# Computing the cross-attention's values in the attention's first batch instead of in the preparation

## The chip, the cores and the metric

The kernel runs on one core of a Trainium2 chip. The metric is the time of one execution on the device in microseconds, the median of several runs. The profile is of one execution; its span runs from the first to the last instruction.

## What is computed

One decoder layer over x of 8 x 512 x 512, with a context of 8 x 77 x 512. Three sublayers stand one behind the other, each with a residual and a layer norm: a mixing of tokens in the frequency domain, a cross-attention with 16 heads onto the context, and a dense layer whose weights are first rounded to 4 bits.

```python
qkv = x @ w_qkv                                     # 8 heads of 64
kv = cumsum(fft(k) * fft(v), axis=1)
x = layernorm(x + ifft(kv * conj(fft(q))).real @ w_out)

q, k, v = x @ W_q + b_q, ctx @ W_k + b_k, ctx @ W_v + b_v     # 16 heads of 32
attn = softmax(where(mask == 0, -1e6, q @ k.T / sqrt(32)))
x = layernorm(x + (attn @ v) @ W_o + b_o)

w = clip(round(kernel / scale), -8, 7) * scale      # scale = max|kernel| / 7
x = layernorm(x + x @ w + bias + (x @ a) @ b)
```

## The kernel before, in words

All matrix products take float32 apart into a high and a low piece, so that a product is three matmuls per 128 rows of the contraction (`split_matmuls`, L130). ScalarE makes the high piece by a copy, VectorE or GpSimd the low one by a subtraction. There are three blocks, each ended by a barrier of all engines. Within a block every engine has its own list of work, written out by hand, and waits on semaphores. All DMAs are issued by SyncE, in the order of its list.

**Preparation** (`prepare`, L134 to L484). TensorE turns the context (616 rows, kept as `ctxT`, two pieces), then makes the keys in 8 products of 308 columns and the values in 5 products of 12 matmuls with 512 columns (4 of 128 rows, `tiles`, and one of 104). ScalarE and VectorE cut each product into its pieces in four slots, `out_hi` and `out_lo`, from which SyncE stores it to DRAM (`keys_split`, `values_split`). A slot is used again once its store has landed. Then come 12 folds: w_qkv is turned and multiplied by the Fourier matrix, which gives `w_spec`, and at the end `w_back` from w_out. A fold's product needs one of two banks, which VectorE frees when it has made the low piece (`split_folded`, L454). Between these, VectorE quantizes the dense layer's weights: the greatest absolute value of `kernel` (L443, behind the fourth value tile), then three passes. After the sixth fold it begins to turn x of the first batch (L92), which it waits for. GpSimd makes the low pieces of W_v.

**Mixing** (`mix_tokens`). 8 batches over two tiles for x. At its end TensorE turns the mixed first batch (`x1`) and projects it to queries, VectorE and GpSimd (`root`, L761) finish the last batch's layer norm, and SyncE loads the first keys.

**Attention** (`attend`). A step is a batch: 8 scores (four tiles of 128 tokens, two halves of the heads), softmax, the turning of the probabilities in three banks per tile (P00 to P32), the turning of the next batch's x1 (X0 to X3) and its queries (Q0 to Q3), and of the batch before: weighing the values (V), W_o (O), turning (T), the dense layer (F). Scores have banks of their own; everything else goes through a ring of 4 banks (`shared_ps`), whose order the lists `START_ORDER` and `BANK_ORDER` give: `Shared` works out from them which bank a use has and which earlier one must be empty (`freed`, counted by VectorE). The first batch (step 0) has only scores, P, X and Q. For a tile ScalarE runs 16 exponentials (`exponentials`, L1413), 8 per half, each half behind VectorE's maximum (L1719, L1724), and the next tile's score in that half waits for them.

SyncE's list in step 0 is: the values of batch 0 (`load_values`, L1114, 12 small DMAs per piece into the block-diagonal `v_block`), then the keys of batch 1 (`load_next_keys`, L517, 8 DMAs), then the residual. The first score of batch 1 waits for these keys:

```python
def load_values(i):
    wait_reuse(sp, oT_hi, i * NC)
    for part in range(2):
        for odd, j, m, row, key, n in v_pieces():
...
...
pe.wait_ge(k_loaded, nth(i, 1, 0) * (16 * 2 * GH))
```

Of the kernel before, what the change touches and what calls it, by code (L numbers as in the profile page):

```python
# [18 lines left out]
F32 = mybir.dt.float32  # L19
# [6 lines left out]
P = 128  # L26
# [20 lines left out]
QMAX = 7.0  # L47

# [85 lines left out]
def prepare(nc, ins, constants, half_power, ident, w_spec, w_back, k_dram, v_dram, ffn_dram, x_first, hand, ffn,  # L134
            out_slots, w_k, w_v):
# [4 lines left out]
    rows = B * KEYS  # L140
    half_rows = rows // 2
    tiles = [(n * P, min(P, rows - n * P)) for n in range((rows + P - 1) // P)]
    tail, tail_rows = tiles[NC]
    with ExitStack() as ctx:  # L144
# [13 lines left out]
        raw_v = wqkv_sb[:].rearrange("p c n -> p (c n)")[:, NC * D:2 * NC * D].rearrange("p (c n) -> p c n", c=NC)  # L158
# [13 lines left out]
        ctx_loaded, wk_loaded, wv_loaded = sem("ctx_loaded"), sem("wk_loaded"), sem("wv_loaded")  # L172
# [4 lines left out]
        wk_hi_ready, wk_lo_ready, wv_hi_ready, wv_lo_ready = sem("wk_hi_ready"), sem("wk_lo_ready"), sem("wv_hi_ready"), sem("wv_lo_ready")  # L177
        prod_ready, prod_used = sem("prod_ready"), sem("prod_used")
        k_biased, k_hi_ready, k_lo_ready = sem("k_biased"), sem("k_hi_ready"), sem("k_lo_ready")
        v_hi_ready, fold_hi_ready = sem("v_hi_ready"), sem("fold_hi_ready")  # L180
        stored = [sem(f"kv_stored{n}") for n in range(SLOTS)]
# [6 lines left out]
        NKEY, NVAL = 2 * NC, len(tiles)  # L188
# [18 lines left out]
        def _(sp):  # L207
# [8 lines left out]
            sp.dma_start(raw_v, by_chunk(ins["W_v"])).then_inc(wv_loaded, 16)  # L216
            sp.dma_start(fwd[:], ins["dft_forward"]).then_inc(fwd_loaded, 16)
            load_interleaved(sp, wqkv_sb, ins["w_qkv"], 0, qkv_loaded[0])
            for n in range(NKEY):
# [6 lines left out]
                if n == NC + 1:  # L226

                    sp.wait_ge(tail_turned, NC)
                    sp.wait_ge(a_turned, 1)
                    sp.dma_start(ffn[:], by_chunk(ins["kernel"])).then_inc(kernel_loaded, 16)  # L230
                elif 1 <= n < NC:

                    sp.wait_ge(wv_lo_ready, NC)
                    load_interleaved(sp, wqkv_sb, ins["w_qkv"], n, qkv_loaded[n])
            for n, (at, size) in enumerate(tiles):
                sp.wait_ge(prod_used, AT_V + n + 1)
                for part, tile in enumerate((out_hi, out_lo)):
                    sp.dma_start(v_dram[part, at:at + size, :], tile[0:size, n % SLOTS, :].bitcast(F32)).then_inc(stored[n % SLOTS], 16)
                if n == 1:

                    sp.wait_ge(wk_lo_ready, NC)
                    sp.dma_start(wout_sb[:], by_chunk(ins["w_out"])).then_inc(out_loaded, 16)

# [11 lines left out]
            for n in range(SLOTS):  # L255
                sp.wait_ge(stored[n], 32 * (NKEY // SLOTS + len(range(n, NVAL, SLOTS))))
# [4 lines left out]
        def _(pe):  # L261
# [29 lines left out]

            pe.wait_ge(wv_hi_ready, 1)
            pe.wait_ge(wv_lo_ready, NC)
            for m, (at, size) in enumerate(tiles):
                n = AT_V + m
                pe.wait_ge(prod_used, n - 1)
                pieces = [([t[:, k, at:at + size] for t in ctxT], [w[:, k, :] for w in w_v]) for k in range(NC)]
                split_matmuls(nc, prod[n % 2][0:size, :], pieces).then_inc(prod_ready, 1)
# [46 lines left out]
        def _(act):  # L345
# [10 lines left out]
            act.wait_ge(wv_loaded, 16)  # L356
            nc.scalar.activation(w_v[0][:], raw_v, ACT.Copy).then_inc(wv_hi_ready, 1)
# [5 lines left out]
            for m, (at, size) in enumerate(tiles):  # L363
                act.wait_ge(prod_ready, AT_V + m + 1)

                act.wait_ge(stored[m % SLOTS], 32 * (NKEY // SLOTS + m // SLOTS))
                nc.scalar.activation(out_hi[0:size, m % SLOTS, :], prod[(AT_V + m) % 2][0:size, :], ACT.Copy).then_inc(v_hi_ready, 1)

# [22 lines left out]
        def _(pool):  # L391
            nc.gpsimd.memset(half_power[:], -0.5)
            pool.wait_ge(wv_loaded, 16)
            pool.wait_ge(wv_hi_ready, 1)
            for c in range(NC):
                nc.gpsimd.tensor_tensor(w_v[1][:, c, :], raw_v[:, c, :], w_v[0][:, c, :].bitcast(F32),
                                        ALU.subtract).then_inc(wv_lo_ready, 1)
# [4 lines left out]
        def _(dve):  # L402
# [31 lines left out]
            for m, (at, size) in enumerate(tiles):  # L434
                dve.wait_ge(v_hi_ready, m + 1)

                dve.wait_ge(stored[m % SLOTS], 32 * (NKEY // SLOTS + m // SLOTS))
                nc.vector.tensor_tensor(out_lo[0:size, m % SLOTS, :], prod[(AT_V + m) % 2][0:size, :],
                                        out_hi[0:size, m % SLOTS, :].bitcast(F32), ALU.subtract).then_inc(prod_used, 1)

                if m == 3:
                    dve.wait_ge(kernel_loaded, 16)
                    nc.vector.tensor_reduce(top[:], ffn[:].rearrange("p c n -> p (c n)"), AX.X, ALU.max,  # L443
                                            apply_absolute_value=True).then_inc(top_ready, 1)
                if m == 4:
# [75 lines left out]
def mix_tokens(nc, x, x1_dram, k_dram, mask_dram, ident, sigma, w_spec, w_back, half_power, w_q_dram, w_q, bias_q, hand):  # L521
# [4 lines left out]
    with ExitStack() as ctx:  # L526
# [50 lines left out]
        def _(sp):  # L577
# [32 lines left out]
            for i in range(B - 3, B - 1):  # L610
                finish(i)
# [144 lines left out]
        def _(pool):  # L756
# [59 lines left out]
            for t in range(NT):  # L816
                root(B - 1, t)
# [1237 lines left out]
```

## Time and profile before

| | |
|---|---|
| median of 3 runs | 937.67 us (936.75 to 938.23) |
| the profiled execution | 939.91 us |
| its span | 937.3 us |
| busy: TensorE / VectorE / ScalarE / GpSimd | 885.3 (94%) / 654.1 (70%) / 369.1 (39%) / 360.4 (38%) |
| mean granted clock of TensorE | 0.978 of full speed |
| bytes written to DRAM / read | 22.87 MB / 52.60 MB |

The execution's own time is 2.6 us more than its span; that part lies outside of what the trace shows. On the trace's clock the preparation ends at about 93 us and the attention block begins at about 456.8 us.

### The profile page before, as it was taken

The page shows a single profiled execution, that of the slowest core. Times are in us where ns is not written, and L with a number is a line of the kernel's source. Part 1 is how long each engine was busy: PE and PEld are TensorE (multiplying, and loading weights), DVE is VectorE, ACT ScalarE, POOL GpSimd, SP SyncE. Part 2 cuts the span into 40 slices and gives each one's busy share as a digit, 9 for nine tenths or more (in the row PEclk, how much of TensorE's full clock was granted, in tenths as well). Part 3 has the DMA queues.
Part 4 walks back from the last instruction along what each step waited for, and adds up shares of the span by engine and source line. Part 5 has one row for each costly group of instructions (what it writes and reads, how often), then busy time and mean ns, then how long its engine had stood idle before and what let it go on. Part 6 is the DMA issues. An engine that isn't in the chain of part 4 may idle for free.

```text
span 937.3 us, 14606 instructions
## 1 busy us (share of the span) xinstructions
PE 885.3 (94%) x4284; PEld 733.8 (78%) x4284; DVE 654.1 (70%) x1133; ACT 369.1 (39%) x1403; POOL 360.4 (38%) x338
## 2 busy tenths in 40 slices
PE   4798999999999999999689999999999999999887
PEld 4683888888888888888578888888888888888775
DVE  2355456666666657567667977879778797887957
ACT  3152221112121211101387555755556646566611
POOL 1000365434353544315236444335443353434523
PEclk9997999999999999999879999999999999999999
DMA  6871720312314020104513141321403114030021
GB/s 184 261 227 45 167 58 34 102 62 74 92 43 133 12 79 23 67 24 133 190 25 99 23 123 31 98 66 25 136 13 96 66 30 134 11 94 18 19 79 45
DMA packets 85962, 76.02 MB, mean 81 GB/s; under 512 B 39895, under 2 KB 58583, under 8 KB 85919
## 3 DMA queue, kind: packets, MB, share of 16 engines
q1 hardware_dynamic: 85919, 75.49, 27.4%
q8 instruction: 21, 0.34, 0.2%
q14 instruction: 22, 0.18, 0.1%
HBM read 52.60 MB, written 22.87 MB: 81 GB/s over the span
## 4 chain that ended last, share of the span: by engine, by line
PE 44%; DVE 5%; issue 2%; ACT 1%; DVEq 0%; POOLq 0%; POOL 0%; ACTq 0%
PE shared_ps L130 33%; PE score_ps L130 5%; PE shared_ps L1206 3%; PE shared_ps L1168 1%; PE shared_ps L1239 1%; DVE xT_lo L1677 1%; DVE score_ps L1719 1%; DVE x_and_res L1765 1%; ACT probs L1413 1%; DVE pT_lo L1704 0%; DVE stats L1749 0%; DVE top_s L1724 0%; DVE y L1743 0%; DVE hidden L1710 0%; DVE y_out L1765 0%
## 5 line engine op out<-in xcount | busy, mean ns | idle before, releaser
L1413 ACT ACTIVATE probs<-score_ps,top_s 128x77 f32<-128x77 f32 x512 | 158.9, 362 | 28.5 <-DVE top_s L1724 28.5
L1413 ACT ACTIVATION_READ_ACCUMULATOR probs<-score_ps,top_s 128x1 f32 x512 | 124.7, 245 | 0.0
L1562 POOL TENSOR_TENSOR probs<-probs,per_total 128x616 f32<-128x616 f32 x64 | 79.1, 1253 | 67.1 <-DVE per_total L1731 66.9
L1555 POOL TENSOR_TENSOR rstd<-ve,half_power 128x1 f32<-128x1 f32 x64 | 35.0, 547 | 154.5 <-DVE ve L1754 149.4
L100 POOL TENSOR_TENSOR xT_lo<-x_tok,xT_hi 128x512 fp32r<-128x512 f32 x28 | 39.0, 1396 | 85.7 <-ACT xT_hi L96 85.7
L729 ACT ACTIVATE qT_hi<-vals 128x512 fp32r<-128x512 f32 x32 | 19.3, 628 | 119.1 <-POOL vals L776 103.8
L776 POOL TENSOR_TENSOR vals<-qs_prod 128x512 f32<-128x512 f32 x32 | 40.9, 1290 | 62.7 <-DVE qs_prod L862 62.7
L1420 ACT ACTIVATE pT_hi<-shared_ps 128x512 fp32r<-128x512 f32 (+1 forms) x96 | 47.6, 539 | 42.0 <-PE shared_ps L1206 41.8
L722 ACT ACTIVATE v_sb<-v_ps 128x512 f32<-128x512 f32 x32 | 18.9, 594 | 106.8 <-PE v_ps L130 106.8
L1577 POOL TENSOR_TENSOR x_and_res<-x_and_res,bias_f 128x512 f32<-128x512 f32 x32 | 41.7, 1302 | 43.9 <-DVE x_and_res L1765 30.1
L1719 DVE COPY_PREDICATED score_ps<-hidden,score_ps 128x616 f32<-128x616 int32 x64 | 50.9, 796 | 10.9 <-PE score_ps L130 10.6
L761 POOL TENSOR_TENSOR mix_rstd<-mix_ve,half_power 128x1 f32<-128x1 f32 x32 | 21.9, 686 | 94.4 <-DVE mix_ve L881 94.4
L1704 DVE TENSOR_TENSOR pT_lo<-shared_ps,pT_hi 128x512 fp32r<-128x512 f32 (+1 forms) x96 | 56.0, 595 | 0.5 <-issue 0.3
L130 PE MATMUL shared_ps<-w_ffn_hi,xT_hi 128*128 128x512 f32 x120 | 49.2, 410 | 7.4 <-DVE xT_lo L1677 6.0
L130 PE MATMUL shared_ps<-w_o_hi,xT_hi 128*128 128x512 f32 x128 | 53.4, 417 | 1.9 <-DVE xT_lo L1685 1.8
L1724 DVE TENSOR_REDUCE top_s<-score_ps 128x8 f32<-128x616 f32 x64 | 51.2, 799 | 3.6
L130 PE MATMUL v_ps<-xT_hi,w_spec_hi 128*128 128x512 f32 x128 | 49.9, 390 | 1.8 <-PEq L144 1.8
L130 PE MATMUL score_ps<-xT_hi,qT_hi 128*128 128x308 f32 x128 | 42.5, 332 | 9.7 <-ACT probs L1413 7.5
L130 PE MATMUL shared_ps<-w_o_lo,xT_hi 128*128 128x512 f32 x128 | 51.0, 398 | 0.0
L130 PE MATMUL shared_ps<-w_o_hi,xT_lo 128*128 128x512 f32 x128 | 50.8, 397 | 0.0
L130 PE MATMUL v_ps<-xT_hi,w_spec_lo 128*128 128x512 f32 x128 | 49.8, 389 | 0.0
L130 PE MATMUL v_ps<-xT_lo,w_spec_hi 128*128 128x512 f32 x128 | 49.8, 389 | 0.0
(210 smaller groups left out, 2637.0 us busy)
## 6 DMA issues: line engine op xcount, KB each, us to landing
x_tok<-in_x SPq DMA_DIRECT2D x32, 256.0 KB, 4.6
x_res<-in_x SPq DMA_DIRECT2D x8, 1024.0 KB, 7.6
x_between<-mix_x SPq DMA_DIRECT2D x32, 256.0 KB, 2.0
x<-x_between SPq DMA_DIRECT2D x8, 1024.0 KB, 5.5
x_tok<-x_between SPq DMA_DIRECT2D x8, 1024.0 KB, 5.6
out<-y_out SPq DMA_DIRECT2D x32, 256.0 KB, 2.0
wqkv_sb<-in_w_qkv SPq DMA_DIRECT2D x16, 192.0 KB, 5.6
keys_split<-w_q_hi SPq DMA_DIRECT2D x8, 154.0 KB, 5.4
```

Source lines behind the costliest of these rows:

```text
L100: engine.tensor_tensor(blocks(xT[1][:, j, :]), block_column(tile, j), blocks(xT[0][:, j, :]).bitcast(F32), ALU.subtract).then_inc(lo_ready, 1)
L130: last = nc.tensor.matmul(out, l, r, start=(n == 0), stop=(n == len(terms) - 1))
L776: nc.gpsimd.tensor_tensor(vals[:, h, :], qs[:, 2 * h, :], qs[:, 2 * h + 1, :], ALU.subtract if h else ALU.add).then_inc(vals_summed, 1)
L1206: last = nc.tensor.transpose(shared_ps[s.bank(use)][0:size, n * P:(n + 1) * P], probs[:, t % 2, at:at + size], ident[:])
L1413: nc.scalar.activation(probs[:, t % 2, j * KEYS:(j + 1) * KEYS], score_ps[:, g, k * KEYS:(k + 1) * KEYS], ACT.Exp, bias=top[:, t % 2, j:j ...
L1420: nc.scalar.activation(pT[0][0:size, first:first + chunks, t * P:(t + 1) * P], turned_bank(s, t, c), ACT.Copy).then_inc(turned_hi, 1)
L1555: nc.gpsimd.tensor_tensor(rstd[:, n:n + 1], ve[:, n:n + 1], half_power[:], ALU.pow).then_inc(rstd_ready, 1)
L1562: nc.gpsimd.tensor_tensor(p, p, per_total[:, t % 2, h * heads:(h + 1) * heads].unsqueeze(2) .to_broadcast([P, heads, KEYS]), ALU.mult).the ...
L1577: nc.gpsimd.tensor_tensor(res2[:, t % 2, :], x2[:, t % 2, :], bias_f[:], ALU.add).then_inc(res2_ready, 1)
L1704: nc.vector.tensor_tensor(lo, turned_bank(s, t, c), hi.bitcast(F32), ALU.subtract).then_inc(freed, 1)
L1719: nc.vector.copy_predicated(s4, hidden[:, t, :].unsqueeze(1).unsqueeze(1).to_broadcast(shape), masked[h].unsqueeze(1).unsqueeze(1).to_broa ...
L1724: nc.vector.tensor_reduce(top[:, t % 2, h * 8:(h + 1) * 8].rearrange("p (g j) -> p g j", j=GH), s4, AX.X, ALU.max, negate=True).then_inc(t ...
```

## The change

Preparation: W_v is no longer loaded or cut apart, and the 5 value products, their copies and their stores are gone. All of w_qkv is loaded at the start, w_out right behind it. The turned context `ctxT`, both pieces, is stored to DRAM (`ctx_turned`, 2 DMAs) behind the last key store and ahead of x. `top` stands before the folds, the scale behind the second fold, the first pass behind the third.

Mixing: W_v is loaded into `x_tok0` before the last batch but one is finished. ScalarE copies its high piece behind the turning of the next x1, GpSimd makes the low pieces in four parts between the last roots. SyncE loads the turned context back (4 DMAs) behind the first keys, into the room of `w_spec`, which now lives on into the attention and holds `w_o`, `w_ffn` and `v_block` too.

Attention, first batch: the value products W0 to W4 take their place in the ring. ScalarE and VectorE cut each into `pT`, SyncE stores it (10 DMAs) and waits until all have landed; then come `load_values` and the keys of batch 1 as before.

```diff
-        AT_V = NKEY
-        AT_FOLD = AT_V + NVAL
+        AT_FOLD = NKEY
...
             sp.dma_start(a_sb, by_chunk(ins["a"])).then_inc(a_loaded, 16)
-            sp.dma_start(raw_v, by_chunk(ins["W_v"])).then_inc(wv_loaded, 16)
             sp.dma_start(fwd[:], ins["dft_forward"]).then_inc(fwd_loaded, 16)
-            load_interleaved(sp, wqkv_sb, ins["w_qkv"], 0, qkv_loaded[0])
+            for r in range(NC):
+                load_interleaved(sp, wqkv_sb, ins["w_qkv"], r, qkv_loaded[r])
+            sp.wait_ge(wk_lo_ready, NC)
+            sp.dma_start(wout_sb[:], by_chunk(ins["w_out"])).then_inc(out_loaded, 16)
...
-            for n, (at, size) in enumerate(tiles):
-                sp.wait_ge(prod_used, AT_V + n + 1)
-                for part, tile in enumerate((out_hi, out_lo)):
-                    sp.dma_start(v_dram[part, at:at + size, :], tile[0:size, n % SLOTS, :].bitcast(F32)).then_inc(stored[n % SLOTS], 16)
+            sp.wait_ge(ctx_hi, 2 * NC)
+            sp.wait_ge(ctx_lo, 2 * NC)
+            for part, tile in enumerate(ctxT):
+                sp.dma_start(ctx_dram[part], tile[:].bitcast(F32)).then_inc(ctx_stored, 16)
...
-            for m, (at, size) in enumerate(tiles):
-                dve.wait_ge(v_hi_ready, m + 1)
...
-                if m == 3:
-                    dve.wait_ge(kernel_loaded, 16)
+            dve.wait_ge(kernel_loaded, 16)
+            nc.vector.tensor_reduce(top[:], ffn[:].rearrange("p c n -> p (c n)"), AX.X, ALU.max,
+                                    apply_absolute_value=True).then_inc(top_ready, 1)
...
+            sp.dma_start(x_tok[0][:], w_v_dram.rearrange("(c p) n -> p c n", p=P)).then_inc(wv_loaded, 16)
+            finish(B - 2)
...
+            sp.wait_ge(q_filled, nth(B - 1, 4, 3))
+            for part in range(2):
+                for into, cols in zip(hand.ctxT(w_spec), (slice(0, S), slice(S, CTX_ROWS))):
+                    sp.dma_start(into[part].bitcast(F32), ctx_dram[part, :, :, cols]).then_inc(hand.ctx_loaded, 16)
             store(B - 1)
...
-START_ORDER = ["P00", "P01", "P02", "X0", "X1", "X2", "X3", "P10", "P11", "P12", "Q0", "P20", "P21", "Q1",
-               "P22", "Q2", "P30", "P31", "P32", "Q3"]
+START_ORDER = ["W0", "W1", "W2", "P00", "P01", "P02", "W3", "X0", "X1", "W4", "P10", "P11", "P12", "X2", "X3",
+               "Q0", "Q1", "P20", "P21", "P22", "Q2", "P30", "P31", "P32", "Q3"]
...
+            for n, (at, size) in enumerate(CTX_TILES):
+                sp.wait_ge(freed, Shared(0, False, True, True).emptied(f"W{n}"))
+                for part in range(2):
+                    sp.dma_start(v_dram[part, at:at + size, :].rearrange("p (a n) -> p a n", a=2),
+                                 values_of(part, n).bitcast(F32)).then_inc(v_stored, 16)
+            sp.wait_ge(v_stored, 32 * len(CTX_TILES))
             step(0, False, True, True)
...
             score(0, s, 0, 0)
             score(0, s, 0, 1)
+            project_v(s, 0)
             score(0, s, 1, 0)
+            project_v(s, 1)
             score(0, s, 1, 1)
-            score(0, s, 2, 0)
+            project_v(s, 2)
             turn_probs(0, s, 0, 0)
             turn_probs(0, s, 0, 1)
             turn_probs(0, s, 0, 2)
+            score(0, s, 2, 0)
+            project_v(s, 3)
             turn_x1(1, s, 0)
+            turn_x1(1, s, 1)
             score(0, s, 2, 1)
-            turn_x1(1, s, 1)
+            project_v(s, 4)
```

How the lists move, first SyncE's in the preparation, from the last value stores on (before) and from the sixth key store on (changed). `w_q_hi` and `w_q_lo` are the slots, `x` is the tile that receives `kernel`, `x_tok` receives x:

```order
L242 DMA wout_sb<-in_w_out 128x4x512
L238 DMA values_split<-w_q_hi 128x512
L238 DMA values_split<-w_q_lo 128x512
L238 DMA values_split<-w_q_hi 128x512
L238 DMA values_split<-w_q_lo 128x512
L238 DMA values_split<-w_q_hi 104x512
L238 DMA values_split<-w_q_lo 104x512
L246 DMA x_tok<-in_x 32x16x128 x4
L249 DMA wqkv_sb<-in_dft_inverse 128x512
```

```order
L233 DMA x<-in_kernel 128x4x512
L226 DMA keys_split<-w_q_hi 128x308
L226 DMA keys_split<-w_q_lo 128x308
L226 DMA keys_split<-w_q_hi 128x308
L226 DMA keys_split<-w_q_lo 128x308
L238 DMA ctx_turned<-ctxT_hi 128x2464
L238 DMA ctx_turned<-ctxT_lo 128x2464
L241 DMA x_tok<-in_x 32x16x128 x4
L244 DMA wqkv_sb<-in_dft_inverse 128x512
```

Where x followed the last value store, it now follows two stores of 1232 KB each that stand directly behind the keys.

ScalarE's list at the attention's start, before and changed. `probs` are the exponentials, `pT_hi<-shared_ps 128x4x128` and `104x2x128` a tile's turned probabilities, `xT_hi` x1 of the next batch, `qT_hi` its queries, and `pT_hi<-shared_ps 128x2x256` (or `104x2x256`) the high piece of a value product:

```order
L1413 ACTIVATE probs,total<-score_ps,top_s 128x77 x40
L1420 ACTIVATE pT_hi<-shared_ps 128x4x128 x2
L1420 ACTIVATE pT_hi<-shared_ps 104x2x128
L1396 ACTIVATE xT_hi<-shared_ps 128x512
L1413 ACTIVATE probs,total<-score_ps,top_s 128x77 x8
L1396 ACTIVATE xT_hi<-shared_ps 128x512 x3
L1420 ACTIVATE pT_hi<-shared_ps 128x4x128 x2
```

```order
L1458 ACTIVATE probs,total<-score_ps,top_s 128x77 x8
L1446 ACTIVATE pT_hi<-shared_ps 128x2x256
L1468 ACTIVATE pT_hi<-shared_ps 128x4x128 x2
L1458 ACTIVATE probs,total<-score_ps,top_s 128x77 x8
L1468 ACTIVATE pT_hi<-shared_ps 104x2x128
L1446 ACTIVATE pT_hi<-shared_ps 128x2x256
L1458 ACTIVATE probs,total<-score_ps,top_s 128x77 x8
L1435 ACTIVATE xT_hi<-shared_ps 128x512 x2
L1446 ACTIVATE pT_hi<-shared_ps 104x2x256
L1458 ACTIVATE probs,total<-score_ps,top_s 128x77 x8
L1468 ACTIVATE pT_hi<-shared_ps 128x4x128 x2
```

The changed piece begins with tile 1's first half of exponentials and the copy of W2; ahead of it stand the two halves of tile 0, each with a value piece behind it (W0, W1). The last value piece (W4, 104 rows) stands behind five halves of exponentials and ahead of the sixth, and all of tile 1's turned probabilities stand behind that.

## Rows read from the trace of the kernel before

**Rows 1.** The page, part 2: TensorE's granted clock, in 40 slices of 23.4 us

```profile
PEclk9997999999999999999879999999999999999999
```

**Rows 2.** Stretches: length, busy us (instructions) by engine, clock, DMA share, GB/s

```profile
40.00:50.00 10.00, 5.26 (x13) 4.16 (x14) 1.57 (x3) 1.09 (x2) 0.00 (x0) 0.66 1.04 367
457.00:500.00 43.00, 32.02 (x153) 27.57 (x154) 28.50 (x46) 32.89 (x149) 12.73 (x11) 0.80 0.30 93
500.00:545.00 45.00, 44.15 (x240) 37.76 (x239) 38.68 (x73) 28.28 (x133) 26.45 (x24) 1.00 0.28 79
```

**Rows 3.** TensorE in the preparation: start, length, line, work, [idle before <- ended by]

```profile
33.71 0.40 PE L130 MATMUL prod<-xT_hi,ctxT_hi 128*128 128x512 f32 x1
...
44.74 0.80 PE L130 MATMUL prod<-xT_hi,ctxT_hi 128*128 128x512 f32 x1 [5.28 <-DVE w_q_lo L438]
...
49.60 0.49 PE L130 MATMUL prod<-xT_lo,ctxT_hi 128*128 128x512 f32 x1
...
55.51 1.04 PE L309 MATMUL turned<-ident,wqkv_sb 128*128 128x128 f32 x8
```

**Rows 4.** VectorE in the preparation, same columns

```profile
32.97 0.48 DVE L432 TENSOR_TENSOR w_q_lo<-wT_sb,w_q_hi 128x308 fp32r<-128x308 f32 x1 [0.23 <-DVE wT_sb L420]
...
54.16 2.27 DVE L443 TENSOR_REDUCE top<-x 128x1 f32<-128x2048 f32 x1
...
58.68 0.69 DVE L454 TENSOR_TENSOR w_spec_lo<-prod,w_spec_hi 128x512 fp32r<-128x512 f32 x1 [1.33 <-ACT w_spec_hi L385]
...
66.78 0.70 DVE L92 STREAM_TRANSPOSE x_tok<-x_tok 128x512 f32<-128x512 f32 x1
```

**Rows 5.** SyncE's queue in the preparation, same columns

```profile
37.88 0.39 SPq L230 DMA_DIRECT2D x<-in_kernel  x1
```

**Rows 6.** Stretches of 2 us in the preparation, same columns as rows 2

```profile
34.00:36.00 2.00, 2.00 (x10) 1.64 (x9) 0.45 (x1) 0.46 (x1) 0.00 (x0) 1.00 1.05 246
46.00:48.00 2.00, 2.00 (x6) 1.52 (x6) 0.00 (x0) 0.00 (x0) 0.00 (x0) 0.50 1.07 390
62.00:64.00 2.00, 2.00 (x20) 2.00 (x20) 0.72 (x2) 1.28 (x3) 0.00 (x0) 1.00 1.24 233
```

**Rows 7.** DMA issues: count, KB each, median us to landing

```profile
values_split<-w_q_lo SPq DMA_DIRECT2D x4, 256.0 KB, 2.8
...
x_tok<-in_W_o SPq DMA_DIRECT2D x1, 1024.0 KB, 5.2
...
xT_lo<-keys_split SPq DMA_DIRECT2D x8, 38.5 KB, 1.9
```

**Rows 8.** TensorE in the attention's first batch and at the second's start

```profile
457.18 0.41 PE L130 MATMUL score_ps<-xT_hi,qT_hi 128*128 128x308 f32 x1 [2.17 <-DVE score_ps L1672]
...
464.10 0.62 PE L130 MATMUL score_ps<-xT_hi,qT_hi 128*128 128x308 f32 x1 [4.94 <-ACT probs L1413]
...
499.92 0.30 PE L130 MATMUL score_ps<-xT_hi,qT_hi 128*128 128x308 f32 x1
```

**Rows 9.** SyncE's queue in the attention's first batch

```profile
461.31 10.49 SPq L1114 DMA_DIRECT2D v_block_hi<-values_split  x12
471.85 9.92 SPq L1114 DMA_DIRECT2D v_block_lo<-values_split  x12
...
487.76 1.85 SPq L517 DMA_DIRECT2D xT_lo<-keys_split  x4
```

**Rows 10.** ScalarE in the attention's first batch: its first exponential

```profile
461.49 0.33 ACT L1413 ACTIVATE probs<-score_ps,top_s 128x77 f32<-128x77 f32 x1 [5.75 <-DVE top_s L1724]
```

**Rows 11.** The mixing's end: ScalarE, GpSimd's last root, VectorE's last piece

```profile
446.89 0.69 ACT L752 ACTIVATE qT_hi<-k_ps,bias_q 128x512 fp32r<-128x512 f32 x1 [7.42 <-PE k_ps L130]
...
450.30 0.80 POOL L761 TENSOR_TENSOR mix_rstd<-mix_ve,half_power 128x1 f32<-128x1 f32 x1 [2.64 <-DVE mix_ve L881]
...
455.77 0.75 DVE L930 SCALAR_TENSOR_TENSOR qT_lo<-q_ps,bias_q,qT_hi 128x512 fp32r<-128x512 f32 x1 [1.97 <-ACT qT_hi L752]
```

**Rows 12.** The page, part 5: GpSimd's subtractions of 128x512 in the mixing

```profile
L100 POOL TENSOR_TENSOR xT_lo<-x_tok,xT_hi 128x512 fp32r<-128x512 f32 x28 | 39.0, 1396 | 85.7 <-ACT xT_hi L96 85.7
```

More of the change, by code:

```diff
@@ L47 @@
 QMAX = 7.0
+CTX_ROWS = B * KEYS
+CTX_TILES = [(n * P, min(P, CTX_ROWS - n * P)) for n in range((CTX_ROWS + P - 1) // P)]
 def nth(batch, per_batch, index):
@@ L131, in split_matmuls, with prepare @@
     return last
-def prepare(nc, ins, constants, half_power, ident, w_spec, w_back, k_dram, v_dram, ffn_dram, x_first, hand, ffn,
-            out_slots, w_k, w_v):
-    rows = B * KEYS
+def prepare(nc, ins, constants, half_power, ident, w_spec, w_back, k_dram, ctx_dram, ffn_dram, x_first, hand, ffn,
+            out_slots, w_k):
+    rows, tiles = CTX_ROWS, CTX_TILES
     half_rows = rows // 2
-    tiles = [(n * P, min(P, rows - n * P)) for n in range((rows + P - 1) // P)]
     tail, tail_rows = tiles[NC]
@@ L815, in _, with split_wv @@
                 nc.gpsimd.memset(tile.bitcast(F32), 0.0).then_inc(hand.keys_cleared, 1)
-            for t in range(NT):
-                root(B - 1, t)
+            def split_wv(c):
+                pool.wait_ge(wv_hi, 1)
+                pool.wait_ge(wv_loaded, 16)
+                nc.gpsimd.tensor_tensor(w_v[1][:, c, :], x_tok[0][:, c, :], w_v[0][:, c, :].bitcast(F32),
+                                        ALU.subtract).then_inc(hand.wv_lo, 1)
+            split_wv(0)
+            root(B - 1, 0)
+            split_wv(1)
+            root(B - 1, 1)
+            split_wv(2)
+            root(B - 1, 2)
+            root(B - 1, 3)
+            split_wv(3)
         @block.vector
@@ L995, in bank @@
     def bank(self, use):
-        return self.order.index(use) % RING
+        shift = 0 if self.order is START_ORDER else len(START_ORDER)
+        return (self.order.index(use) + shift) % RING
     def filled(self, use):
@@ L1180, in project_q, with project_v @@
                 split_matmuls(nc, shared_ps[s.bank(use)][:], pieces).then_inc(filled, 1)
+            def project_v(s, n):
+                use, (at, size) = f"W{n}", CTX_TILES[n]
+                if n == 0:
+                    pe.wait_ge(hand.wv_lo, NC)
+                    pe.wait_ge(hand.ctx_loaded, 16 * 4)
+                wait_reuse(pe, freed, s.reusable(use))
+                ctx_of = ctx_main if n < NC else ctx_rest
+                at = at % S
+                pieces = [([x[:, k, at:at + size] for x in ctx_of], [w[:, k, :] for w in w_v]) for k in range(NC)]
+                split_matmuls(nc, shared_ps[s.bank(use)][0:size, :], pieces).then_inc(filled, 1)
             def score(i, s, t, h):
```

194 lines of the change are left out of this document (105 added, 89 removed).

## The prediction

> **What bounds the kernel now.** I read the clock and the stretches first, then TensorE's list with its idle time, then the lists of those that ended it. TensorE is busy for 94% of the span, and its clock falls in the preparation's second half (the slice from 70 to 94 us) and at the change from mixing to attention (445 to 492 us) [rows 1]; from 40 to 50 us it was 0.66 too [rows 2]. In the attention's first batch it is busy for 32.0 of 43 us at a mean clock of 0.80; in the 45 us after that it is idle for 0.85 us [rows 2]. So what delays the second batch's start delays the end by as much, and what fills the first batch's holes is partly free. In the preparation the value products run from 33.71 to 55.51 us, where the first turning for the folds begins: 21.8 us, of which 5.28 us are a wait for a slot whose store is late, and the 12 matmuls after it ran at half clock, 44.74 to 49.9 us [rows 3], while the DMA engines moved 367 GB/s [rows 2]. The preparation then hangs on VectorE: its first fold piece is at 58.68 us, its first turning of x, behind the sixth fold, at 66.78 us, and it did not wait for x [rows 4]. From there to the block's end the lists are the same in both kernels.
>
> The bound of measurement is 0.2%, 1.9 us: below that I call it no change.
>
> **Term 1: the preparation.** The question is when VectorE can turn x. Three things lead there.
>
> (a) The keys. TensorE ends them at about 33.9 us as before. Their last slots waited for stores behind the w_qkv loads before; now these loads are issued first. The sixth low piece ends at 32.97 + 0.48 = 33.45 us [rows 4], and behind its two stores (0.8 us of issue) the load of `kernel` is issued at 34.4 instead of 37.88 us [rows 5]. The last key piece should be done at 35.6 us.
>
> (b) The maximum. A load of 1 MB that had company landed after 5.2 us [rows 7]; with two key stores ahead I add 1 us: 40.6 us. The maximum takes 2.27 us [rows 4], so 42.9 us. TensorE has made folds 0 and 1 by then and stands still from about 39.4 to 43.7 us, since VectorE has freed no bank. That is a wait like the one of 5.28 us, which left the clock at half for 4.9 us of matmuls (44.74 to 49.60) [rows 3]. At half clock a fold takes about 2.6 us, so two of them, and then two at the 1.35 us of the list before ((66.78 - 58.68) / 6): folds 0 to 5 are done at about 51.5 us.
>
> (c) x. It stands behind, from 34.4 us on, one pair of key stores not yet moved (0.32 MB), `kernel` (1.05), two more pairs (0.63) and the context's stores (2.52): 4.5 MB. At the 367 GB/s of the value stores' time [rows 2] they take 12.3 us, then x's 1.05 MB at the 233 GB/s of x's own loading [rows 6] 4.5 us, and 2 us until the last has landed (the 2.8 us of a value store less 0.7 us for its 256 KB) [rows 7]: 53.2 us.
>
> So x decides, at 53.2 instead of 66.78 us: **13.6 us less**. From both sides: with everything ahead of x at 246 GB/s [rows 6], 59.2 us and 7.6 us less; with 390 GB/s [rows 6] and no tail, x lands at 50.4 us, and the folds at full clock are done at 50 us: 16.4 us less. I take the middle rate, since the context's stores are nearest to the value stores, in direction and in size.
>
> **Edits I cost at nothing.** The 1 MB of W_v and 2.5 MB of context that are loaded while the mixing ends move beside TensorE, which is saturated there. The context is issued behind the first keys, at about 444 us; at 233 GB/s with 2 us of tail it lands at 457 us, and its first reader, W0, can start at 459. If that cover were gone, each microsecond past 461 would count. GpSimd's four parts of W_v (1.4 us each, [rows 12]) stand between the roots; the last root began at 450.30 us and the block ended with VectorE at 456.52 us [rows 11], so over 5 us of slack stand against at most 2 us of shift. ScalarE's copy falls in its 7.42 us without work ahead of its first piece of the queries [rows 11]. The residual of batch 6, now behind W_v in SyncE's queue, is read only in the middle of the next step.
>
> **Term 2: the attention's first batch.** Added are 60 matmuls at 0.2325 us (12 in 2.8 us, [rows 3] before the stall), 14.0 us, five copies on ScalarE and five pieces on VectorE (0.7 us each at most, as a piece of a fold, [rows 4]), ten stores and a wait on SyncE. Now the list: scores of tile 0 from 457.18 us [rows 8], done at 459. W0 until 461.7. The next score waits for the eight exponentials that begin at 461.49 [rows 10], until 464.1 as before [rows 8], 2.6 us a half; W1 to 467.8, score, W2 to 471.4, three turnings to 473.3, score, W3 to 477.0, X0, X1, score to 478.8, **W4 to 481.6**. ScalarE's copy ends at 482.4; VectorE stands in the maximum of tile 2's second half until 483.8 and frees W4 at 484.4. Two exits lead from there to the second batch.
>
> The keys: the last store is issued at 485.0 and lands after 2.8 us [rows 7], 487.8. Then the 24 value loads, 10.49 + 9.92 us of issue before, now at least 9.92 twice [rows 9]: 508.0. Then 8 key loads, 3.7 us, the last landing 1.9 us after its issue began [rows 7, 9]: **513.2 us**. Before, these 20 us began at 461.31 us and nobody waited for the keys, which had been issued by 489.6.
>
> TensorE's own way: tile 1's turnings, a score, X2 and X3, which need banks that VectorE frees only behind the sixth half of exponentials: TensorE is nearly idle from 485 to 492 us, so that Q0's 12 matmuls run at half clock, as in [rows 3]. Q0 to 497.4, score, Q1, tile 2's turnings, Q2, and tile 3's probabilities behind its own exponentials; Q3 ends at about 512.5 us.
>
> Both give 513, against 499.92 us for the second batch's first score before [rows 8]: **13.4 us more**. Bounds: if the chain to W4 were 3 us shorter and TensorE's holes smaller, 10 us more; if W4 is freed 3.5 us later, 17. Below, a perfect filling of the 11 us of holes and of the slow clock would cost nothing, but the keys' chain excludes it: even a W4 that is freed at 479 us gives 507.8, 8 us more.
>
> The Trainium skill, DMA: Bandwidth & Descriptors, "Issuing engines are not separate DMA queues", says that the time an engine needs to start a DMA is usually small beside the DMA. By that rule the keys would be there before 495 us, TensorE's own way would decide alone, and the term would be 12.6 instead of 13.4 us. The trace does not agree: here a DMA of 19 KB holds the queue for 0.85 us.
>
> **The sum.** -13.6 + 13.4 = -0.2 us on the span, 937.3 to 937.1; the profiled execution was 2.6 us longer than its span and 2.2 us above the median. On the median of 937.67: **937.5 us**.
>
> **The rivals.**
> - Faster. The DMA engines keep up: the context's stores run at 390 GB/s, x lands at about 51 us, and the first batch is not as slow, since value products between the scores keep the clock up and W4 is freed at 481.5: -15.6 + 10.5 = -5.1, 932.6 us. For it: the clock of 0.80 there [rows 2] and a first score that found a cold engine. Against: TensorE's hole at 485 to 492 us stays. The Trainium skill, TensorE: Matmul & The Clock Gate, "Why this matters for your kernels", asks for no idle gaps between bursts of matmuls; by that rule it would come out this way, and the 5.28 us gap with its slow matmuls agrees with it.
> - Slower. SyncE's chain takes the place of the slot wait: its 20 us of small loads now begin only when all five value tiles have landed. If W4 is freed 3.5 us later than I count, the keys land at 516.7 us; TensorE, done at 512.5, then waits 4.2 us, and the second batch starts at half clock, which costs 2.2 us as after the 5.28 us gap (4.9 us for what takes 2.8). -13.6 + 16.8 + 2.2 = +5.4, 943.1 us. It decides from the point at which the keys land 3.5 us behind Q3.
> - The products do not find their cover: the context lands only at about 464 us, behind x1's stores, and W0 holds up the second tile's score in TensorE's list: +2.5 us, 940.0 us.
>
> **How the numbers follow.** My forecast 0.33, faster 0.33, slower 0.30, late context 0.04. The two terms are opposed, of equal size, and each is known to 3 us, so the likeliest has its own range of 934.5 to 940.5. The range of 931 to 944 us takes in both rivals and their bounds but not term 1's 7.6 us. Of my forecast's 0.33, 0.25 lies within 0.2%, 0.04 on each side; the near ends of the rivals give 0.01 and 0.02 more: faster 0.36, same 0.28, slower 0.36.
>
> **What would show it.** VectorE's first turning of x at 53 us with a wait for x in front; no slot waits; the maximum at 40.6 us; the mixing unchanged in length; W4 freed at 484.4 us after the attention's start of 456.8 (27.6 us later); the value loads as a solid row of 20 us on SyncE's queue and, right behind, the keys; the second batch's first score 56 us behind the first score instead of 42.7. It is wrong if x waits for nothing, if that distance is under 52 or over 60 us, or if any stage after it changes its length.

## The result, and the profile after

The changed kernel takes 944.00 us (median of 4 runs, 942.05 to 944.52) against 937.94 us for the kernel before (4 runs, 936.75 to 938.23): 1.0057 times as long, 95% interval 1.0045 to 1.0070. Beside the experiments below it ran again, 941.79 us against 937.98: 1.0047, interval 1.0031 to 1.0064. So it is **slower, by 4 to 6 us**; the forecast was 937.5.

The first trace has a span of 942.7 us against 937.3. Four marks that both kernels have cut it into stages. TensorE's list gives three of them in the changed kernel (start, duration, engine, line, operation, tile, shape, count, idle time before it and what ended it):

```profile
81.32 0.47 PE L134 MATMUL v_ps<-xT_hi,w_spec_hi 128*128 128x512 f32 x1 [1.83 <-PEq L147]
...
446.29 0.41 PE L134 MATMUL score_ps<-xT_hi,qT_hi 128*128 128x308 f32 x1 [3.89 <-DVE score_ps L1725]
...
503.27 0.63 PE L134 MATMUL score_ps<-xT_hi,qT_hi 128*128 128x308 f32 x1 [3.63 <-DMA xT_lo<-keys_split]
```

They are the mixing's first product, the attention's first score and the second batch's first score. The fourth is the first load of the third batch's keys on SyncE's queue, at 538.33 us before and here at

```profile
544.24 1.76 SPq L501 DMA_DIRECT2D xT_hi<-keys_split  x4
```

In the kernel before, the mixing's first product is at

```profile
93.96 0.47 PE L130 MATMUL v_ps<-xT_hi,w_spec_hi 128*128 128x512 f32 x1 [1.83 <-PEq L144]
```

and the two scores at 457.18 and 499.92 [rows 8]. The lengths, in us:

| stage | before | after | difference | forecast |
|---|---|---|---|---|
| preparation, to the mixing's first product | 93.96 | 81.32 | -12.64 | -13.6 |
| mixing, to the attention's first score | 363.22 | 364.97 | +1.75 | 0 |
| first batch, to the second's first score | 42.74 | 56.98 | +14.24 | +13.4 |
| from there to the third batch's keys | 38.41 | 40.97 | +2.56 | 0 |
| rest of the span | 398.97 | 398.46 | -0.51 | 0 |
| span | 937.30 | 942.70 | +5.40 | -0.2 |

The two terms I had worked out are each within a microsecond. Most of the miss, 4.3 us, stands in two of the stages that I had put at nothing.

**Preparation.** VectorE's list after, to be held against [rows 4]:

```profile
41.47 2.29 DVE L411 TENSOR_REDUCE top<-x 128x1 f32<-128x2048 f32 x1 [5.58 <-DMA x<-in_kernel]
...
54.01 0.71 DVE L96 STREAM_TRANSPOSE x_tok<-x_tok 128x512 f32<-128x512 f32 x1 [1.14 <-DMA x_tok<-in_x]
```

The slot waits are gone, the maximum stands at 41.5 instead of behind the value products, and the first turning of x at 54.0 instead of 66.78, behind a wait for x.

**Mixing's end.** SyncE's queue, and the next write of VectorE into the two-tile buffer that x1's stores empty:

```profile
429.32 2.91 SPq L501 DMA_DIRECT2D xT_lo<-keys_split  x4
432.27 0.67 SPq L615 DMA_DIRECT2D w_spec_hi<-ctx_turned  x1
...
434.32 0.76 SPq L615 DMA_DIRECT2D xT_lo<-ctx_turned  x1
435.12 9.55 SPq L580 DMA_DIRECT2D x_between<-mix_x  x4
```

```profile
442.65 0.55 DVE L897 TENSOR_SCALAR mix_x<-mix_r,mix_mv,mix_rstd 128x512 f32<-128x512 f32 x1 [5.05 <-DMA x_between<-mix_x]
```

The four loads of the context are issued just ahead of x1's last stores. The first store's 256 KB stand behind 2.5 MB, and VectorE cannot write the third normalised tile before they have gone. One more tile and three remainders of the queries are queued behind that instruction; the last of them ends at 445.6 us. TensorE had ended its own list at 442.4 us: its wait before the first score is 3.89 us against 2.17 [rows 8].

**First batch and second batch's start.** SyncE's queue:

```profile
472.67 1.02 SPq L1171 DMA_DIRECT2D values_split<-pT_hi  x1
473.74 0.89 SPq L1171 DMA_DIRECT2D values_split<-pT_lo  x1
477.91 20.02 SPq L1130 DMA_DIRECT2D w_spec_lo<-values_split  x24
497.98 1.92 SPq L501 DMA_DIRECT2D xT_hi<-keys_split  x4
499.94 1.87 SPq L501 DMA_DIRECT2D xT_lo<-keys_split  x4
```

The solid row of 20 us is there, with the keys behind it. TensorE is done at 499.64 us and waits 3.63 us for them (the row at 503.27 above), and then runs at a slow clock. The stretches of the changed kernel (busy time and count of PE, its weight loads, DVE, ACT, POOL; then the granted clock, DMA share, GB/s):

```profile
503.00:509.00 6.00, 5.73 (x18) 4.91 (x19) 1.60 (x2) 0.17 (x1) 4.06 (x5) 0.55 0.91 330
509.00:520.00 11.00, 10.93 (x54) 9.15 (x53) 7.30 (x11) 8.29 (x43) 5.92 (x5) 1.00 0.11 29
```

The kernel before, in the first 6 us of its second batch:

```profile
500.00:506.00 6.00, 6.00 (x33) 5.21 (x32) 5.33 (x8) 3.66 (x18) 5.85 (x4) 1.00 0.62 192
```

At a granted clock of 0.55 (mostly the lower level, 1.2 of 2.4 GHz) TensorE starts 18 matmuls in 6 us instead of 33. The filler below shows that this is the +2.56 us.

### The profile page after: what moved, and what is told of

Its sections match the earlier page's. It is cut to its first block, busy times and chain, and to the rows that moved or that the text cites. A ratio compares the mean times of both kernels' runs of the same rounds, so it can differ in the third digit from the quotient of the medians.

```text
span 942.7 us, 14604 instructions
## 1 busy us (share of the span) xinstructions
PE 884.1 (94%) x4284; PEld 733.3 (78%) x4284; DVE 654.9 (69%) x1133; ACT 369.2 (39%) x1403; POOL 360.2 (38%) x338
## 4 chain that ended last, share of the span: by engine, by line
PE 43%; DVE 4%; SPq 2%; issue 2%; ACT 1%; DMA 1%; POOLq 0%; POOL 0%; DVEq 0%
PE shared_ps L134 33%; PE score_ps L134 5%; PE shared_ps L1240 3%; SPq L1130 2%; PE shared_ps L1191 1%; PE shared_ps L1273 1%; DVE xT_lo L1730 1%; DVE x_and_res L1825 1%; ACT probs L1458 1%; DVE score_ps L1779 1%; DMA values_split<-pT_lo 0%; DVE pT_lo L1764 0%; SPq L501 0%; DVE stats L1809 0%; DVE y L1803 0%
## 5 line engine op out<-in xcount | busy, mean ns | idle before, releaser
L134 PE MATMUL shared_ps<-w_spec_hi,xT_hi 128*128 128x512 f32 (+1 forms) x380 | 139.1, 408 | 9.7 <-DVE xT_lo L1730 6.4
L134 PE MATMUL shared_ps<-w_spec_hi,xT_lo 128*128 128x512 f32 (+1 forms) x252 | 99.4, 394 | 0.0
L134 PEld LDWEIGHTS shared_ps<-w_spec_hi,xT_hi 128*128 128x128 f32 (+1 forms) x380 | 72.1, 190 | 28.1 <-issue 6.6
L134 PE MATMUL shared_ps<-pT_hi,w_spec_lo 128*128 128x512 f32 x192 | 61.5, 402 | 0.1
L134 PEld LDWEIGHTS shared_ps<-w_spec_hi,xT_lo 128*128 128x128 f32 (+1 forms) x252 | 47.7, 189 | 8.6
L134 PE MATMUL shared_ps<-xT_hi,w_q_hi 128*128 128x512 f32 x112 | 46.8, 418 | 5.1 <-DVE xT_lo L1730 3.2
L134 PE MATMUL v_ps<-xT_lo,w_spec_hi 128*128 128x512 f32 x128 | 49.8, 389 | 0.0
```

Source lines behind the costliest of these rows:

```text
L134: last = nc.tensor.matmul(out, l, r, start=(n == 0), stop=(n == len(terms) - 1))
```

## The experiments

Each kernel ran beside the kernel before on the same chip; ratios are to that one. Distances are those of the table: P (preparation), M (mixing), F (first batch), G (from there to the third batch's keys).

**Context ahead of the keys** (from the changed kernel):

```diff
-            sp.wait_ge(hand.keys_cleared, 2)
-            load_keys(sp, k_dram, hand, 0)
-
             sp.wait_ge(q_filled, nth(B - 1, 4, 3))
             for part in range(2):
...
+            sp.wait_ge(hand.keys_cleared, 2)
+            load_keys(sp, k_dram, hand, 0)
             store(B - 1)
```

> The changed kernel with the reload of the turned context moved ahead of SyncE's wait for the cleared keys. Theory: in the changed kernel the 2.5 MB of context stand in the DMA queue ahead of x1's last four stores, VectorE then waits 5.05 us for a store to land before it can write the third normalised tile, and the attention begins 1.75 us later than it should. Then that wait goes, the distance from the mixing's first value product (81.32) to the attention's first score (446.29) falls from 364.97 to about 363.2 us as before, and the time falls by 1.7 us, to about 942.3. Rival: the extra 1.75 us come from GpSimd's four parts of W_v or ScalarE's copy; then nothing changes, 944.0.

940.21 us, 1.0029 (1.0014 to 1.0044), about 2 us under the changed kernel (the ratios say 1.7 to 2.6). The first context load is now issued at 419.33, and VectorE's third tile waits for no store:

```profile
437.98 0.55 DVE L898 TENSOR_SCALAR mix_x<-mix_r,mix_mv,mix_rstd 128x512 f32<-128x512 f32 x1
439.10 1.37 DVE L898 TENSOR_SCALAR mix_x<-mix_r,mix_mv,mix_rstd 128x512 f32<-128x512 f32 x1
```

TensorE's wait before the first score is 2.16 us again. M is 364.32 in this trace, not 363.2, but the excess lies earlier: from x1's first turning on TensorE (424.58) to the first score (445.00) it is 20.42 us, as in the kernel before (436.77 to 457.18, 20.41), against 22.14 in the changed kernel (424.15 to 446.29). In the five later kernels with this edit M is 363.23 to 363.27. Shown: the context's place in the queue costs the 1.7 us, not GpSimd's or ScalarE's work on W_v, which is unchanged.

**Early value loads.** The first batch reads only 77 rows of the values, all among the 128 of W0, so its 24 loads need not wait for W4 (the first halves now follow the store of W0, the second halves that of W3):

```diff
+                if n == 0:
+                    sp.wait_ge(v_stored, 32)
+                    load_values(0, (0,))
+                if n == 3:
+                    load_values(0, (1,))
             sp.wait_ge(v_stored, 32 * len(CTX_TILES))
```

> The changed kernel, but the first batch's value loads wait only for the store of W0 (they read its rows alone): first halves behind W0's store, second halves behind W3's. Theory: the 20 us of value loads behind W4's store make the second batch's keys late; now the keys are issued before 490 us, TensorE does not wait 3.63 us for them and does not start the second batch at half clock: second batch's first score about 53.4 us behind the first score instead of 56.98, and 2.5 us more from the clock: -6.1 us, about 937.9. Rival: TensorE's own way or VectorE decides next, and the clock's part comes from something else: -3.6 us at most, 940.4.

938.60 us, 1.0008 (0.9992 to 1.0024): some 4 us gained, between the 6.1 of the theory and the 3.6 of its rival. SyncE issues the keys at 486.81, and the second batch starts without a wait and at full clock:

```profile
499.99 0.30 PE L134 MATMUL score_ps<-xT_hi,qT_hi 128*128 128x308 f32 x1
```

G is 38.47, as before the change, so the clock's part of the theory held (2.50 us). F is 54.60, 2.4 us less than in the changed kernel, and TensorE's own way sets it now, as the rival said. F was to be 53.4; most of the rest is Q2, which in this trace began at half clock after 1.99 us without work (first matmul 0.79 us instead of 0.50).

**A filler for the wait.** The wait for the keys stays, but TensorE works through it:

```diff
+                if isinstance(i, int) and i == 1 and t == 0 and h == 0:
+                    pe.wait_ge(exped, i * (NT * XH) + ((t - 1) * XH + (h + 1) * XH // 2))
+                    for _ in range(26):
+                        nc.tensor.matmul(score_ps[:, 0, 0:GK], w_q[0][:, 0, 0:P], x1T[0][:, 0, 0:GK], start=True, stop=True)
                 if t == 0:
```

> The changed kernel with 26 matmuls of 308 columns put into a free score bank ahead of the second batch's wait for its keys (their result is overwritten). The keys are as late as before. Theory: the 2.56 us by which the second batch's start is longer is TensorE's half clock after the idle 3.63 us; with the engine kept busy the clock stays at full, the second batch's first score stands where it did (503.3) and the time falls by 2.5 us, to about 941.5. Rival: the second batch is longer for another reason (late values, VectorE): 944.0 or a little more.

942.26 us, 1.0048 (1.0030 to 1.0065). By the totals alone this is no gain that can be told from the changed kernel's 1.0047 and 1.0057. The trace tells it apart:

```profile
499.58 3.81 PE L1221 MATMUL score_ps<-xT_hi,w_q_hi 128*128 128x308 f32 x26
503.23 0.38 PE L134 MATMUL score_ps<-xT_hi,qT_hi 128*128 128x308 f32 x1
```

The true score begins at 503.23, directly behind the filler (F is 57.49: the keys' last loads were issued 0.4 us later behind the first score than in the changed kernel, and the filler may have held the score for another 0.1 us). The next matmuls take 0.30 us instead of 0.46, and G is 541.79 - 503.23 = 38.56 instead of 40.97 (38.41 before). So the slow start is the clock after the idle time, but for 0.15 us; in the kernel's total the 2.4 us are partly lost in the scatter from run to run.

**Both edits.**

> The context ahead of the keys and the early value loads together. If the two costs are independent they add: -1.7 - 6.1 = -7.8, about 936.2 us, 1.7 us below the kernel before. If they are not (an attention that starts earlier meets its W_o and x1 loads later), about 938.

937.54 us, 0.9988 (0.9974 to 1.0003): the gains that the two runs measured, 2 and 4 us, add, and the change is back at the kernel before. The 936.2 counted on the 6.1 us that the value loads alone had not given. M 363.24, F 52.59, G 38.40.

**The changed kernel again, and W4 moved.** The kernel with W4 moved starts from the one with both edits. It has four edits of one kind: in TensorE's list W4 moves from behind tile 2's scores to between X3 and Q0, and in the bank order, ScalarE's and VectorE's lists with it.

```diff
-START_ORDER = ["W0", "W1", "W2", "P00", "P01", "P02", "W3", "X0", "X1", "W4", "P10", "P11", "P12", "X2", "X3",
+START_ORDER = ["W0", "W1", "W2", "P00", "P01", "P02", "W3", "X0", "X1", "P10", "P11", "P12", "X2", "X3", "W4",
```

> The changed kernel itself, beside the variants on the same chip. Every theory expects the distances of its first trace: second batch's first score 57 us behind the attention's first, 41 us from there to the third batch's keys, and a time 0.57% above the kernel before, about 6 us behind it.

The changed kernel again: P 79.78, M 364.57, F 57.00, G 40.14 at 1.0047. The picture is the same, but G was to be 41 and the time 0.57% longer: here the clock was still full for the first matmuls after the wait of 3.95 us and fell behind them, which cost 1.7 us instead of 2.56.

> Context ahead of the keys, early value loads, and W4 moved behind X3, into the 3.07 us in which TensorE waits for X3's remainder. Theory: with the keys out of the way TensorE's own list sets the second batch's start, so W4's 2.8 us vanish in the hole, and Q0 runs at full clock instead of half (2.4 us): the second batch's first score comes 52.6 - 2.8 - 2.4 = 47.4 us behind the first instead of 52.6, and the time is 4 to 5 us under that of the version without the move, about 932.5 to 933.5. Rival: ScalarE's exponentials of tile 3 set the pace (they are followed by the last probabilities and Q3); then under 2 us are gained, 936.

W4 moved: 935.97 us, 0.9979 (0.9968 to 0.9990). F is 51.69, 0.9 us less than without the move, not 5: the gain is as small as the rival said. Q0 did run at full clock, but W4 only filled a hole that another one replaced (TensorE now waits 4.24 us ahead of X3, and W4's first matmuls run at half clock), and Q2 still waits for the bank of Q1, whose copy stands behind the last exponentials on ScalarE:

```profile
473.18 1.11 PE L1197 MATMUL shared_ps<-ident,x 128*128 128x128 f32 x4 [4.24 <-DVE pT_lo L1770]
...
487.38 0.50 PE L134 MATMUL shared_ps<-xT_hi,w_q_hi 128*128 128x512 f32 x1 [2.01 <-DVE qT_lo L1744]
```

> The version above with x's four loads ahead of the context's stores in the preparation. Theory: in the changed kernel VectorE waits 1.14 us for x, and the context's 2.5 MB stand ahead of x in the queue; then that wait goes and the preparation ends 1.1 us earlier. Rival: the folds and the quantising of the ffn weight hold VectorE anyway, and nothing changes (less than 0.4 us).

W4 moved and x first: 934.44 us, 0.9968 (0.9953 to 0.9982). The wait for x is gone (its turning at 54.44 waits for nothing), yet from the maximum's start to the mixing's first product it is 39.81 us against 40.05. The pair further below settles it: no gain.

**Thin products.** From the changed kernel; of each value product one matmul of 12 is left, so the values are only one part of their sum; every copy, store, load and wait stays.

```diff
-                split_matmuls(nc, shared_ps[s.bank(use)][0:size, :], pieces).then_inc(filled, 1)
+                nc.tensor.matmul(shared_ps[s.bank(use)][0:size, :], pieces[0][0][0], pieces[0][1][0], start=True, stop=True).then_inc(filled, 1)
```

> The changed kernel with each value product cut to one of its 12 matmuls (the values are then only one part of the sum; every copy, store, load and wait stays): 55 matmuls, 12.8 us of TensorE, are gone. Theory: the second batch waits for SyncE's chain behind W4, not for TensorE; W4 is freed at the pace of the exponentials, at most 3 us earlier, so the second batch starts 54 to 57 us behind the first score and the time falls by 3 us at most, to 941 or more. Rival: TensorE's added matmuls are the cost; then the time falls by 10 us or more, to 934 or less.

940.35 us, 1.0025 (1.0011 to 1.0039): 12.8 us of TensorE's work taken out give about 2 us, not 10. F is 55.13:

```profile
499.79 0.62 PE L134 MATMUL score_ps<-xT_hi,qT_hi 128*128 128x308 f32 x1 [4.57 <-DMA xT_lo<-keys_split]
```

TensorE is done at 495.22, that is 50.6 us behind the first score, against 53.35 with the full products. So of the 10.6 us by which its own way is longer than the 42.74 before, taking out the matmuls gives back under 3, net of what their absence costs: in the thin kernel TensorE waits up to 2.50 us between the first scores, and tile 0's turnings run at half clock. The rest must lie in the order, in the copies, or in both. In the order this stands out, before and after:

```profile
484.71 0.39 PE L130 MATMUL score_ps<-xT_hi,qT_hi 128*128 128x308 f32 x1
```

```profile
484.77 0.31 PE L134 MATMUL score_ps<-xT_hi,qT_hi 128*128 128x308 f32 x1
```

The last half of tile 3's scores began 27.5 us behind the first score in the kernel before, ahead of Q0, and begins 38.5 us behind it after the change, behind Q0. From there to TensorE's end of the batch it is 15.2 us before, 14.9 after, 14.9 here and 14.7 with W4 moved.

**The last score earlier** (from the kernel with W4 moved):

```diff
             turn_x1(1, s, 2)
+            score(0, s, 3, 1)
             turn_x1(1, s, 3)
             project_v(s, 4)
             project_q(1, s, 0)
-            score(0, s, 3, 1)
...
-            split_q(1, s, 0)
             exponentials(0, 3, 1)
+            split_q(1, s, 0)
...
-            split_v(s, 4)
             softmax_top(0, 3, 1)
+            split_v(s, 4)
+            invert_totals(0, 3)
             split_q(1, s, 0)
...
-            invert_totals(0, 3)
```

> The version with W4 in the hole, and the last half of tile 3's scores moved from behind Q0 to between X2 and X3 on TensorE, its exponentials ahead of Q0's copy, and the reciprocals of tile 3 ahead of Q0's remainder. Theory: what sets the end of the first batch is the distance from that score to the second batch's first score, 15 us in every trace; in the kernel before it stands 27.5 us behind the attention's first score, in the changed kernel 38.5, since it waits behind Q0. It can run at about 28.5; the second batch then begins 47 to 48 us behind the first score instead of 51.7, the time is 4 us lower, 932. Rival: TensorE's matmuls and the copies for them fill the time; then 51 us and no gain.

**930.28 us, 0.9923 (0.9907 to 0.9939): faster than both kernels**, by 7.9 us against the one before. F is 48.85, 2.84 us less than with W4 moved; the forecast was 4. The score runs 28.4 us behind the first one, and from there on TensorE never waits over 0.5 us:

```profile
471.91 0.48 PE L134 MATMUL score_ps<-xT_hi,qT_hi 128*128 128x308 f32 x1 [3.02 <-ACT probs L1464]
...
484.86 0.50 PE L134 MATMUL shared_ps<-xT_hi,w_q_hi 128*128 128x512 f32 x1 [0.48 <-DVE qT_lo L1744]
...
489.49 0.50 PE L134 MATMUL shared_ps<-xT_hi,w_q_hi 128*128 128x512 f32 x1 [0.50 <-DVE qT_lo L1744]
```

The 15 us behind this score are 20.4 now: it no longer sets the end, TensorE's own work does. The medians with and without the move differ by 5.7 us (the ratios by 5.2), which is more than the stage gained. P, M and G are the same within 0.1 us; what the two traces differ in beside F is the closing stretch, 108.4 against 111.5 us, which has the same list in both (the last section has its reason). So 2.8 us are shown for the move. Against the kernel before it is -12.5 (P) + 6.1 (F) = -6.4 us, and another 1.6 us less in the closing stretch.

> The version above with x's loads ahead of the context's stores. Theory: 0.4 us or less, nothing that can be told from the version above. Rival: the 1.5 us that the pair with the other order of the scores differed by shows again.

With x first: 930.20 us, 0.9914 (0.9897 to 0.9931); the intervals overlap and the medians differ by 0.1 us. From the maximum's start to the mixing's first product it is 39.83 us against 39.55. Where x's loads stand does not matter. F is 48.96, and 52.01 with x first and the old order of the scores: the move is worth 3.05 us in this pair, whose closing stretches agree (108.4 and 108.3 us).

> The changed kernel with the last half of tile 3's scores ahead of X3 and nothing else (context and value loads as in the change). Theory: SyncE's chain behind W4 decides here, so the second batch's first score stays 57 us behind the first; TensorE is done some 4 to 6 us earlier and waits 8 us or more for the keys, and the second batch starts at half clock as before: no gain, within 1 us of the changed kernel. Rival: it gains 4 us here too.

The last score moved in the changed kernel: 943.38 us, 1.0049 (1.0033 to 1.0065): no gain. F is 56.39, and TensorE waits longer instead:

```profile
503.70 0.62 PE L134 MATMUL score_ps<-xT_hi,qT_hi 128*128 128x308 f32 x1 [6.62 <-DMA xT_lo<-keys_split]
```

TensorE is done 49.8 us behind the first score, 3.6 us earlier than in the changed kernel (4 to 6 were expected), and waits for the keys all the same (6.62 us, where 8 or more were expected). So the same move is worth 2.8 to 3.05 us of F with the key loads out of the way, and at most the 0.6 us that F is shorter without: in the changed kernel SyncE's chain sets F. M is 366.53 in this trace, 1.6 us more than in the changed kernel's first one; all of that lies ahead of x1's first turning, and the granted clock of the mixing's first 10 us was 0.83 here, 1.00 there.

**The kernel before again.**

> The kernel before, for a second trace of its preparation. Every theory expects the mixing's first value product at 94 us within 1 us and the attention's first score 363.2 us behind it; the traces of the changed kernel and its variants, whose preparations differ in nothing but x's place, lay between 79.8 and 81.6.

The kernel before again: P 92.40 (93.96 in the first trace), M 363.23, F 42.74, G 38.40. P was expected within 1 us of 94 and missed by 1.6: it scatters, already at the keys' pieces near 28 us. The changed kernel and its variants have 79.8 to 81.6 in twelve traces, middle 80.7; against the middle of the two before, 93.2, the preparation gained 12.5 us.

## Why the prediction was wrong, step by step

- **Term 1, (a) and (b)**: right. `kernel` was issued at 34.73 (forecast 34.4), the maximum began at 41.47 (40.6), TensorE lost its clock in the wait.
- **Term 1, (c)**: in the first trace x decided, by 1.14 us, at 54.01 instead of 53.2. The term was -12.6 in the first pair of traces and -12.5 over all, against -13.6. With x's loads moved forward VectorE still turned x 12.8 us after the maximum's start, against 12.5, and with x in its place the wait for x was 0.36 and 0.49 us in two later traces, against 1.14 in the first. So the folds were nearly as late as x: the 51.5 us for them was the optimistic number.
- **"Edits I cost at nothing"**: this step failed. I asked whether the context reaches W0 in time, and it does. I did not ask what stands behind it in SyncE's queue: x1's four stores, on which VectorE's two-tile buffer hangs. A store that is behind 2.5 MB cost 1.75 us. The late-context rival named those stores too, but had them ahead of the context, and put the price on W0; TensorE's list shows no wait at W0.
- **Term 2, the keys' chain**: right in mechanism and nearly in size. W4 was freed 26.4 us behind the first score (forecast 27.2). The last pair of stores took 5.2 us from its issue to its landing instead of 3.4, the 24 loads 20.02 as forecast, and F came out at 56.98 against 56. The page cited there, the Trainium skill's DMA: Bandwidth & Descriptors, "Issuing engines are not separate DMA queues", calls the time to start a DMA usually small; by that rule the keys would have been there before 495 us. The trace has them at 503: here 24 loads of 0.2 to 19 KB hold the queue for 20 us, 0.83 us each (the 0.85 us that the forecast gives for 19 KB is this mean over all sizes).
- **Term 2, "TensorE's own way"**: mis-sized, and the wait that came of it is the largest single part of the miss. I had it done at 512.5, 0.7 us ahead of the keys; that is 55.3 us behind the first score. It was done at 53.35: Q0 ended 38.5 us behind the first score and not 40.2, and the list behind it took no longer than I thought. So the wait was 3.63 us, just over the 3.5 us from which the "slower" rival decides, and the second batch began at half clock: +2.56, where the rival had said 2.2. The forecast set two nearly equal arrivals against each other and gave nothing to the wait between them. It did not decide the sign alone: without the 2.56 us the span would still be 2.8 us longer than before, by the mixing's 1.75 us and the two small misses.
- **The rivals.** "Slower" named the mechanism and, with 943.1, the time, but through a W4 that is late, and W4 was early; and it had no loss in the mixing. That its time came out was luck. "Faster" counted on products that keep the clock up. The Trainium skill, TensorE: Matmul & The Clock Gate, "Why this matters for your kernels", asks for no idle gaps. In the trace the products did close the early ones (the wait of 4.94 us [rows 8] is 0.64), but the wait ahead of an x1 turning stayed (2.55 us, 2.47 before), and the change made new ones at Q0 (3.16), Q2 (1.97) and the keys (3.63).
- **What I had in the list and did not price**: the new order puts the last half score behind Q0 ("Q0 to 497.4, score, Q1"). I costed the products' matmuls (14 us) as what lengthens TensorE's way; thin products show that taking them out gives back under 3 us of it. Moving that score alone took 3.6 us off TensorE's way. How the remainder divides between copies and order no run shows.

Summed: +1.0 (term 1) + 1.75 + 0.8 (term 2) + 2.56 - 0.5 = 5.6 us above the forecast's span, 942.7 against 937.1.

## What to carry to other kernels

When a transfer is hidden beside a busy engine, look at what is queued behind it on the same queue, above all stores that free a small buffer. Where two paths are forecast to arrive within a few microseconds of each other, price the wait between them, with the clock after it. And take the last link of a softmax chain, its last score, as early as its inputs allow: moving matmuls into holes took 0.9 us off the first batch, moving that one score 2.8 to 3.05, and only once the queue no longer decided.

## What was unexpected of the hardware

The granted clock after a short idle time is not the same from trace to trace. In the closing stretch all kernels have the same list, and the product F at its end finds TensorE idle for 1.70 us each time. In the kernel with both edits it was slow, in the changed kernel not:

```profile
884.71 0.77 PE L134 MATMUL shared_ps<-w_spec_hi,xT_hi 128*128 128x512 f32 x1 [1.70 <-DVE xT_lo L1736]
885.28 0.63 PE L134 MATMUL shared_ps<-w_spec_hi,xT_lo 128*128 128x512 f32 x1
```

```profile
893.04 0.47 PE L134 MATMUL shared_ps<-w_spec_hi,xT_hi 128*128 128x512 f32 x1 [1.70 <-DVE xT_lo L1730]
893.35 0.40 PE L134 MATMUL shared_ps<-w_spec_hi,xT_lo 128*128 128x512 f32 x1
```

From the eighth batch's keys to the end the fourteen traces took 108.3 to 111.6 us, in three groups, and the waits of TensorE in that stretch are the same in all. They differ in the granted clock at two places: this product F, and the product O 18 us behind it, which finds TensorE idle for 1.77 us. Where the clock stayed at full through both (five traces), the stretch took 108.3 to 108.4 us. Where it fell in one of them (six traces; a granted clock of 0.66 to 0.68 over the 5 us from F's start, or 0.72 over the 6 us from O's), it took 109.9 to 110.1; where it fell in both (three traces), 111.5 to 111.6. So each fall costs about 1.6 us. What decides whether it falls, no run shows; the two traces of the kernel before lie in one group, and so do the two of the changed kernel. Totals here differ by up to 3 us for this alone, and so an effect of 2 us, such as the filler's, is read from the stage and not from the total.
